# Moving the units whose exponentials VectorE computes, in a fused attention and MLP layer

## What is computed

```
q, k = (rotary(q, N), rotary(k, N))
ql, kl = (q @ U, k @ U)
att = jnp.einsum('bhnr,bhmr->bhnm', ql, kl) / math.sqrt(dk)
y = jax.nn.softmax(att, axis=-1) @ v
```

## Time and profile before

| | |
|---|---|
| median of three runs | 2543.27 us |
| the profiled execution | 2545.08 us |
| its span, first to last instruction | 2543.3 us |
| granted TensorE clock, mean of the span | 0.991 |
| TensorE busy | 2471.2 us (97%) |
| ScalarE busy | 1979.6 us (78%) |
| VectorE busy | 1868.9 us (73%) |

### The profile page before, as it was taken

One profiled execution on the slowest core, in us unless ns is written; L12 is line 12 of the kernel. 1 busy time (PEld: TensorE's weight loads), 2 busy tenths in 40 slices (PEclk: granted clock), 3 DMA queues, 4 the chain that ended last, 5 costly groups with the idle time before them and its releaser, 6 DMA issues.

```text
span 2543.3 us, 41712 instructions
## 1 busy us (share of the span) xinstructions
PE 2471.2 (97%) x15898; PEld 1080.6 (42%) x15898; DVE 1868.9 (73%) x2672; ACT 1979.6 (78%) x2190; POOL 56.7 (2%) x105
## 2 busy tenths in 40 slices
PE   3999999999999999999999999999999999999998
PEld 2222222222222222222222222222258888888886
DVE  7377774688888888888888888888645565646563
ACT  2899999999999999999999999999943222322222
POOL 1001000200000000000000000000100000000000
PEclk8899999999999999999999999999999999999999
DMA  3566664843323334333333333334610100111000
GB/s 99 127 150 150 153 152 96 168 78 78 71 59 74 69 62 75 69 64 73 64 66 72 69 67 72 61 71 86 127 36 1 26 10 15 25 25 25 0 9 18
DMA packets 100963, 178.73 MB, mean 70 GB/s; under 512 B 31432, under 2 KB 57064, under 8 KB 100782
## 3 DMA queue, kind: packets, MB, share of 16 engines
q1 hardware_dynamic: 88718, 150.92, 28.9%
q0 software_dynamic: 10336, 23.53, 4.4%
q10 hardware_dynamic: 1728, 1.87, 0.2%
HBM read 150.73 MB, written 25.49 MB: 69 GB/s over the span
## 4 chain that ended last, share of the span: by engine, by line
PE 75%; ACT 12%; issue 9%; DVE 2%; DMA 1%; ACTq 0%; DVEq 0%; SPq 0%
PE PS L762 28%; PE PS L1304 18%; PE PS L731 17%; ACT PB L822 11%; PE PS L1289 5%; PE PS L1316 2%; PE PS L747 2%; ACT EXP L822 1%; DVE accS L1052 1%; PE PS L482 1%; PE PS L478 1%; PE PS L487 0%; PE PS L472 0%; PE PS L1267 0%; DMA KSL<-KSD 0%
## 5 line engine op out<-in xcount | busy, mean ns | idle before, releaser
L822 ACT ACTIVATE PB<-PS 128x1024 f32<-128x1024 f32 x1802 | 1689.7, 1088 | 27.6 <-PE PS L731 22.4
L762 PE MATMUL PS<-PB,V 128*17 128x512 f32 x7208 | 950.3, 599 | 10.5 <-DVE accS L1052 9.7
L731 PE MATMUL PS<-QSL,KSL 49*128 49x512 f32 x3850 | 789.5, 454 | 10.7 <-DMA KSL<-KSD 7.4
L731 PEld LDWEIGHTS PS<-QSL,KSL 49*128 49x128 f32 x3850 | 347.7, 184 | 784.2 <-ACT PB L822 650.9
L1383 ACT ACTIVATE hfr<-PS,s 128x512 f32<-128x512 f32 x128 | 86.9, 689 | 300.5 <-PE PS L1304 300.4
L828 DVE TENSOR_SCALAR EXP<-PS 128x512 f32<-128x512 f32 x246 | 169.9, 691 | 120.2 <-PE PS L747 114.3
L762 PEld LDWEIGHTS PS<-PB,V 128*17 128x17 f32 x7208 | 119.6, 95 | 307.4 <-issue 222.0
L1304 PE MATMUL PS<-hidden_ar,wh1r 128*128 128x512 f32 x1024 | 237.6, 391 | 0.0
L1304 PE MATMUL PS<-hidden_br,wh2r 128*128 128x512 f32 x1024 | 235.3, 390 | 0.0
L1304 PEld LDWEIGHTS PS<-hidden_br,wh2r 128*128 128x128 f32 x1024 | 191.7, 188 | 39.4
L1304 PEld LDWEIGHTS PS<-hidden_ar,wh1r 128*128 128x128 f32 x1024 | 190.6, 188 | 40.2 <-DVE hfr L1476 1.0
(11 more groups left out here) (184 smaller groups left out, 1594.1 us busy)
## 6 DMA issues: line engine op xcount, KB each, us to landing
KSL<-KSD SPq DMA_DIRECT2D x255, 256.0 KB
KSL<-KSD SPq DMA_DIRECT2D x255, 128.0 KB
QSD<-qhl SPq DMA_DIRECT2D x32, 256.0 KB
QSL<-QSD SPq DMA_DIRECT2D x62, 132.0 KB
KSD<-khl SPq DMA_DIRECT2D x58, 128.0 KB
first_y<-in_mlp POOLq DMA_DIRECT2D x22, 256.0 KB, 5.7
first_x<-in_mlp POOLq DMA_DIRECT2D x22, 256.0 KB, 6.3
xg<-in_x SPq DMA_DIRECT2D x8, 512.0 KB, 6.7
```

Of the source, the lines that this page charges most:

```text
L731: ins = pe.matmul(PS[:, 2 * (pair % SLOTS) + e, :], KSL[r, q % 2, s, k * P:(k + 1) * P], QSL[r, b % 2, s, :], start=True, stop=True, tile_ ...
L762: ins = pe.matmul(ACC[i * VW:i * VW + DK + 1, :], V17[:, HT * h + u, c, :], probs[:, (i % 2) * QW:(i % 2 + 1) * QW], start=kt == 0, stop=k ...
L822: act.activation(probs, PS[:, slot:slot + 2, :].rearrange("p a b -> p (a b)"), ACT.Exp).then_inc(at["probs_ready"], 1)
```

## The change

The table LATE_AT is rewritten, and one read is moved on VectorE.

```diff
-LATE_AT = {7: ((-3, 1), (-1, 1), (7, 3)), 13: ((3, 1), (6, 0), (13, 3)), 19: ((11, 0), (12, 0), (19, 3)),
-           23: ((15, 0), (18, 0), (24, 3)), 31: ((21, 0), (23, 2), (31, 3))}
+LATE_AT = {7: ((-5, 1), (0, 2), (7, 3)), 13: ((3, 1), (6, 0), (13, 3)), 19: ((10, 0), (11, 2), (19, 3)),
+           25: ((18, 3), (19, 1), (25, 3)), 31: ((23, 1), (24, 2), (31, 3))}
+
+READ_LAST = 19
...
-            if k + 1 < len(LATE):
+            if k + 1 < len(LATE) and unit % KT != READ_LAST:
 
                 late_head_dve(v, k + 1, 0)
             s.did(v.scalar_tensor_tensor(y, y, POW2[2], ee, ALU.add, ALU.mult))
...
             v.scalar_tensor_tensor(late_dve[k % 2], y, POW2[5], et, ALU.add, ALU.mult).then_inc(poly_ready, 1)
             v.wait_ge(poly_ready, k + 1)
+            if k + 1 < len(LATE) and unit % KT == READ_LAST:
+                late_head_dve(v, k + 1, 0)
```

## The result

The changed kernel takes 2571.7 us (median of four runs, 2567.72 to 2576.27) against 2543.41 us before (four runs, 2542.70 to 2545.31): a ratio of 1.0108 [1.0096, 1.0120], so it is slower by 28.3 us. The forecast was slower by 12.2, with 2566 as the upper end of the range. The direction is right, the size isn't.

A forecast was written before the change was run, and what follows sets the result against it. ScalarE and TensorE were taken as nearly full, ScalarE losing 0.63 us per block to late scores. -0.33 - 0.28 + 1.1 = +0.49 per block, 25 times, gave +12.2 us: 2557.3 profiled, 2555.5 median; range 2540 to 2566.

The forecast's parts named there:

- the stall at unit 19: Unit 19: TensorE stands still 1.0 us before head 1 of unit 25, until VectorE has read head 0.
- -0.33: Block's end: head 1 of unit 7, moved from unit 31 to unit 0, hides in idle time; -0.33 us per block.
- -0.28: Units 23 to 31: late unit 23 becomes 25, with sums in its own iteration; -0.28 us per block.
- +1.1: Behind unit 19: ScalarE's fifth exponential after unit 18 ends at e + 5.69, due at e + 4.58; +1.1 us per block.
- Cost nothing: Key loads for heads scored one unit earlier, and for the next block's first keys: in time, no cost.
- The 0.05 between VectorE's end and TensorE's start: Unit 19: hand-over after the read of head 0, 0.05 us of the 1.35 from head 0 to head 1.
- cold behind head 1 too, +1.2: Bound at unit 19: if TensorE must also start cold behind head 1, the loss is +1.2 us per block.
- I say the 0.33 lost there goes: Units 31 to 7: moving head 1 of unit 7 recovers ScalarE's whole loss, 0.33 us per block; bounds -0.33 and 0.
- The cover of 1.4 us: Head 0 of unit 19, at unit 10: key load issued 7.4 us ahead, needs 6.0, leaving 1.4 us.
- The rival that had keys late in their cover: Worse than forecast: late keys, late VectorE or unit 7's head each add 0.2 to 0.4 per block; 2561 to 2566; chance 0.15.
- VectorE's cover of 0.3 us: Unit 25: VectorE's read and polynomial need 0.5 + 9.5 us, TensorE reaches the sums after 10.3; 0.3 us to spare.
- READ_LAST at nothing: Unit 19: head 0 of 25 read behind the polynomial; VectorE waits some 3 us from spare time, at no cost.

The follow-up runs named there:

- the trip alone: Kernel before with only unit 19's heads moved, to (11, 3) and (12, 1), and head 0 read behind unit 13's polynomial: 2572.29 us.
- Moving the weights' loads: Changed kernel with GpSimd's loads of MLP weights starting at unit 500 (block 15) instead of unit 205 (block 6): 2571.31 us.
- the version with later heads: Changed kernel with head 0 of unit 7 and both heads of unit 19 put back where the kernel before has them: 2568.74 us.
- the version with the read in the middle: Changed kernel with READ_LAST 99 instead of 19, so head 0 of unit 25 is read in the middle of unit 19's polynomial: 2666.86 us, one run.
- the other table: Kernel before with LATE_AT rewritten: units 7, 14, 20, 23 and 31 late, other places for their heads: 2549.6 us.

## Why the forecast was right and wrong

The direction was forecast, and so was its cause, the stall at unit 19. What failed is the sum: all three of its terms were mis-sized (-0.33 was -0.24, -0.28 was -0.19, +1.1 was +1.27), and the keys, put at "Cost nothing", were late in block 6. By themselves the ordinary blocks, 25 × 0.84 = 21.0 us, would give 2564.3 by the prediction's way of counting, still below its 2566. Beyond that went, in the main, block 6 (2.5 us on top of an ordinary block's 0.84) and 5.7 us between profiled execution and median.

**The stall, right in kind, short in size.** "TensorE stands still for 1.0 us", "+1.1 per block": 25 waits are there, the sums of 19 and the scores of 20 do stand behind head 1, and the trip alone in the other kernel costs 1.07. In the changed kernel it costs 1.27. The sum went from head 0: 1.35 + 0.32 + 0.98 + 0.50 + 0.05 + 1.02 = 4.22 to the end of ScalarE's next exponential. Measured: 1.44 from head to head (971.57 to 973.01), 0.40 to the sums, 0.98 to the scores, 0.55 to ScalarE's start (974.94), then 1.02: 4.39. Two terms are off. The 0.05 between VectorE's end and TensorE's start was taken from sums behind a transpose, and a head took 0.14. And head 1 itself took 0.40 until its successor, not 0.32, as a score pair took 0.44 and not 0.34 behind a wait. The second was named in the bounds ("cold behind head 1 too, +1.2"), the first in none of them. The steps ahead of head 0 were right to the hundredth: it started 1.47 after the end of unit 18's last exponential (970.10 to 971.57).

**"-0.33 per block" was -0.24.** The head is hidden in full, as the equal 1.08 us show. The loss that it was held responsible for wasn't all its own: 0.09 stays. The step that failed is "I say the 0.33 lost there goes": a cost (the head's 0.32) and a loss (ScalarE's 0.33) were set equal because the numbers were alike. It also comes 24 times and not 25, since block 6 has no late unit 7.

**"-0.28 per block" was -0.19.** The two sums in a row are gone, and 0.09 is still lost between 25 and 31. Same error as above. The rest is not the head of the next unit 7 at unit 27: with that head at unit 29 the loss stays 0.10. What makes it was not tried. The Trainium skill (TensorEngine Tiling, Tiling Modes, Key Properties) says that a change of the tiling mode drains TensorE. One more pair of such changes per block stands in the changed kernel, and this half of the block became faster by 0.19 all the same, so no run here shows a price for them; what the pair costs by itself was not measured.

Together the ordinary block: -0.24 - 0.19 + 1.27 = +0.84, measured +0.84; forecast -0.33 - 0.28 + 1.1 = +0.49. Each of the three terms is off in the same direction, and 24 blocks make 8.4 us of it.

**Key loads: "Cost nothing" was wrong.** The cover of 1.4 us was counted to the last bytes and in block 22 of before, where nothing else uses the queues (and four units at 1.83 are 7.3, not 7.4). The rival that had keys late in their cover put it at 0.2 to 0.4 in every block; in fact it is nothing in 20 blocks, and much in those where GpSimd's transfers run (block 6 lost 3.4 us in all against an ordinary block's 0.84, block 7 lost 1.09) and a little in 21 to 23. Moving the weights' loads shows that they are the cause of 1.8 us in block 6 and of the excess in block 7. The rest in block 6 is open, and so is why 21 to 23 were touched, where none run.

**VectorE's cover of 0.3 us** was right (0.33), and decided two experiments.

**READ_LAST at nothing** was right, with VectorE's wait at 3.4 us ("some 3").

**Profiled execution and median.** I took the 1.8 us between them over to the changed kernel. There the median is 4.0 on the other side of the profiled run. Its runs spread by 8.6 us, those of before by 2.6. Late keys would do that, and the version with later heads spreads by 1.8; but the trip alone, which leaves the heads of unit 7 as they were, spread by 6.4. The mean granted clock of the four runs goes with their times: 0.992 at 2567.72, 0.991 at 2571.58 and 2571.83, 0.990 at 2576.27. One stretch of 6.8 us at 0.50, as other versions show behind a wait, takes 0.0013 off the mean, and in the version with the read in the middle it cost a block some 2.8 us (60.2 against 57.4). So such stretches, of which the profiled execution has none in the blocks with late units, could explain the gap. The slower runs have no trace, and this stays open.

## What to carry to other kernels

Two operations that share one buffer through another engine need the whole round trip between them, and it is twice as long as the middle operation: here 1.44 us around a read of 0.69. Place them so that other work of that length lies between, and then look at who reads the second one: what was saved on the first engine came back in part, twice, as a late polynomial. A loss at a place and the cost of an instruction there aren't the same number; undo one at a time before adding them up. And a transfer that is hidden in the middle of a kernel must be looked at in the blocks where another queue is busy.

## What the runs showed that I had not expected

- **The hand-over back to TensorE depends on what starts.** From VectorE's end it took 0.05 us to sums (705.73 to 705.78, and the earlier trace rows), but 0.14 to a head. An earlier weight load is not the reason: the trace has the sums' first one at 705.78, with their matmul, and the head's at 972.98, already 0.11 after VectorE's end. The reason is open.
- **A stand-still can cost the clock.** With some 1.1 us of stand-still at unit 19 the granted clock stayed at 1.00 in ordinary blocks. With that and 1.83 us more it fell to half for 3.4 or 6.8 us in 24 of 25 blocks, and an ordinary block grew by some 3.4 or 4.7 us over the changed kernel's, for 1.83 us of added wait; in the 25th it didn't fall, and the block grew by 1.90. Single waits of 1.90 (block 16 with the weights' loads) and 2.22 us (block 6 with the other table) were followed by such stretches too, of 3.4 and 6.8 us.
- **One place in a table was worth 10.6 us.** That was head 1 of unit 25, at (19, 3) instead of (19, 1). Another was worth 4.5: the kernel that does nothing but move head 1 of unit 7 to (0, 2) takes 2539.1 us where the kernel before takes 2543.62.
